# Selective scan of a hybrid layer: building the scan's input from a doubled product, its first column written by ScalarE

## The reference

```python
xz = x @ in_proj_w
xb, zb = jnp.split(xz, 2, axis=-1)
xb = silu(causal_conv4(xb) + conv_b);  zb = silu(zb)
x_dbl = xb @ x_proj_w                 # 128 columns for dt, 16 for B, 16 for C
dt = softplus(dt @ dt_proj_w + dt_proj_b)
decay = jnp.exp(dt[..., None] * A)    # A is [2048 channels, 16 states]
inp = dt[..., None] * Bm[:, :, None, :] * xb[..., None]
h = decay_t * h + inp_t               # recurrence over the 2048 tokens
y = sum_n h * C;  y = y + xb * D
out = (y * zb) @ out_proj_w
```

## Time and profile before

| | us |
|---|---|
| median of 2 runs (6987.1 and 7003.95) | 6995.53 |
| the profiled execution | 7032.75 |
| its span on the slowest core (core 3) | 7031.2 |
| spans of the 8 cores | 6956.0 to 7031.2 |
| first to last scan instruction (starts) | 355.5 to 4000.3 |

### The profile page before, as it was taken

How to read it: one execution, slowest core, us unless ns; L and a number is a source line. 1 busy time by engine, 2 the same in 40 slices (tenths; PEclk the granted TensorE clock), 3 DMA queues, 4 the chain that set the end, 5 groups by cost and what they waited for, 6 DMA issues and landing times.

```text
span 7031.2 us, 35693 instructions; the slowest of 8 cores (6956.0 to 7031.2 us)
## 1 busy us (share of the span) xinstructions
PE 2641.7 (38%) x9120; PEld 949.0 (13%) x9120; DVE 3363.1 (48%) x3380; ACT 1385.9 (20%) x2282; POOL 391.0 (6%) x204
## 2 busy tenths in 40 slices
PE   2322214222114222132111200497833434337978
PEld 1100001000001000010000000143311111113433
DVE  0366673566773666745777540101155565652111
ACT  0122221222221222212222202212110101001120
POOL 1000000000000000000000011000002222120000
PEclk8655556655557555565555555698966666668987
DMA  6400004100002000011000169531400000002313
GB/s 106 73 10 9 2 0 68 36 9 8 0 0 60 23 12 2 0 39 33 0 0 0 24 103 118 85 77 41 91 0 0 0 0 0 0 0 33 75 44 100
DMA packets 691337, 226.18 MB, mean 32 GB/s; under 512 B 680122, under 2 KB 680253, under 8 KB 687552
## 3 DMA queue, kind: packets, MB, share of 16 engines
q1 hardware_dynamic: 555552, 168.14, 10.4%
q0 software_dynamic: 135584, 55.76, 7.1%
HBM read 241.73 MB, written 37.88 MB: 40 GB/s over the span
## 4 chain that ended last, share of the span: by engine, by line
DVE 37%; PE 26%; ACT 14%; DMA 10%; issue 6%; DVEq 4%; POOL 1%; ACTq 1%; SPq 0%; POOLq 0%; PEldq 0%
DVE AR L723 17%; ACT AR L695 10%; PE ps L955 7%; PE ps L925 6%; DVE AR L709 5%; DVE AR L1091 4%; PE ps L470 3%; DVEq L58 3%; DVE AR L1127 3%; PE ps L1154 2%; DVE AR L511 2%; PE ps L308 2%; PE ps L1058 2%; DMA AR<-w 1%; POOL AR L1140 1%
## 5 line engine op out<-in xcount | busy, mean ns | idle before, releaser
L747 PE MATMUL ps<-AR 128*128 128x512 bf16 x1024 | 518.2, 608 | 2459.3 <-DVE AR L739 2459.3
L723 DVE TENSOR_TENSOR_SCAN AR<-AR 128x1024 bf16<-128x1024 f32 x512 | 1173.5, 2292 | 40.0 <-issue 3.1
L695 ACT ACTIVATE AR<-AR 128x511 f32<-128x511 f32 x1024 | 674.1, 705 | 1.6 <-issue 1.1
L709 DVE TENSOR_TENSOR AR<-AR 128x1024 bf16<-128x1024 bf16 x512 | 354.5, 692 | 527.3 <-ACT AR L695 519.4
L925 PE MATMUL ps<-AR 128*128 128x512 bf16 x2048 | 474.7, 395 | 119.7 <-DVE AR L343 111.7
L732 ACT ACTIVATE AR<-AR 128x2 f32<-128x2 bf16 x512 | 104.6, 204 | 1962.4 <-DVEq L63 1962.4
L955 PE MATMUL ps<-AR 128*128 128x512 bf16 x2048 | 471.9, 396 | 14.8 <-DMA AR<-w2s 14.8
L962 DVE TENSOR_SCALAR AR<-ps,AR 128x1024 f32<-128x1024 f32 x32 | 43.0, 1344 | 896.8 <-PE ps L955 896.8
L747 PEld LDWEIGHTS ps<-AR 128*128 128x128 bf16 x1024 | 69.7, 104 | 2897.2 <-issue 2897.2
L1154 PE MATMUL ps<-AR 128*128 128x512 bf16 x512 | 220.5, 586 | 636.4 <-POOL AR L1140 609.6
L739 DVE TENSOR_TENSOR AR<-AR 128x1024 bf16<-128x1024 bf16 x512 | 354.4, 692 | 125.9 <-issue 125.9
(11 more groups left out here) (92 smaller groups left out, 2212.8 us busy)
## 6 DMA issues: line engine op xcount, KB each, us to landing
AR<-w1s SPq DMA_DIRECT2D x128, 256.0 KB, 3.0
AR<-w2s SPq DMA_DIRECT2D x32, 1024.0 KB, 6.6
AR<-ip_bf SPq DMA_DIRECT2D x96, 256.0 KB, 2.9
AR<-bc_hbm SPq DMA_DIRECT2D x4, 4096.0 KB, 14.2
AR<-op_bf SPq DMA_DIRECT2D x24, 512.0 KB, 4.7
X<-x_fm SPq DMA_DIRECT2D x1, 8192.0 KB, 28.6
AR<-in_proj_w POOLq DMA_DIRECT2D x32, 256.0 KB, 5.1
ip_bf<-AR SPq DMA_DIRECT2D x32, 256.0 KB, 3.0
```

Source lines behind the costliest of these rows:

```text
L695: nbase=nbase: e.activation(out=dec_all[gb][:, n, 1:TQ], in_=dt[b][:, 1:TQ], func=AF.Exp, scale=av[:, dd, nbase + n:nbase + n + 1]),
L709: e.tensor_tensor(out=inp_all[0], in0=v[b].unsqueeze(1) .broadcast_to([128, G, TQ]), in1=bbc[:, nbase:nbase + G, :], op=ALU.mult))
L723: e.tensor_tensor_scan(out=h_all[hb].rearrange("p a b -> p (a b)"), data0=dec_all[gb].rearrange("p a b -> p (a b)"), data1=inp_all[0].rear ...
L747: e.matmul(self.bank(b, TQ), self.ident[:], hc_all[hb][:, n, :], start=(ng == 0 and n == 0), stop=(ng == NG - 1 and n == G - 1)),
```

## The change

- `v` becomes `vdup`, [128, 2, 512] in bf16: L664 writes its first half, a drain and a copy (VectorE) write the second. `inp` gets two buffers, used in turn by the parity of the group.
- In the prologue VectorE now waits for `bc_done` ahead of L664. Behind L677 come two more operations of 16 elements, each with drains: `B[0] * v[0]` and its sum with `seedv`. So `seedv` now holds the whole of column 0 for all 16 states.
- In a group the multiplication covers columns 1 to 511 of both states only, with `vdup` and B both plain rows of 511 at an offset of one element. It no longer waits for the decays nor for the carry. The addition of 2 elements and its drain are gone. ScalarE, behind its two Exp, copies two elements of `seedv` into column 0 of `inp`, and the scan waits for that copy alone (`col0_done`), which stands behind the Exp in ScalarE's queue.
- `yv` becomes bf16, so L761 has bf16 operands only.

```diff
-        yv = [self.view(o_yv + i * TQ * 4, F32, [128, TQ]) for i in (0, 1)]
+        yv = [self.view(o_yv + i * TQ * 2, BF16, [128, TQ]) for i in (0, 1)]
...
+                r.wait("ve", "d_spb", bc_done)
                 r.op("ve", lambda e, dd=dd, b=b: e.tensor_tensor(
-                    out=v[b], in0=dt[b], in1=xbs[:, dd, :], op=ALU.mult))
+                    out=vdup[b][:, 0, :], in0=dt[b], in1=xbs[:, dd, :],
+                    op=ALU.mult))
+                r.drain("ve")
+                r.op("ve", lambda e, b=b: e.tensor_copy(
+                    out=vdup[b][:, 1, :], in_=vdup[b][:, 0, :]))
...
-                sv_[b] = r.op("ve", lambda e, dd=dd, b=b: e.tensor_tensor(
+                r.op("ve", lambda e, dd=dd, b=b: e.tensor_tensor(
                     out=seedv[b], in0=dec0s[b],
-                    in1=self.carry[:, dd * 16:dd * 16 + 16], op=ALU.mult),
+                    in1=self.carry[:, dd * 16:dd * 16 + 16], op=ALU.mult))
+                r.drain("ve")
+                r.op("ve", lambda e, b=b: e.tensor_tensor(
+                    out=dec0s[b], in0=bbc[:, 0:16, 0],
+                    in1=vdup[b][:, 0, 0:1].broadcast_to([128, 16]),
+                    op=ALU.mult))
+                r.drain("ve")
+                sv_[b] = r.op("ve", lambda e, b=b: e.tensor_tensor(
+                    out=seedv[b], in0=seedv[b], in1=dec0s[b], op=ALU.add),
                               inc="c_ve")["c_ve"]
+                r.drain("ve")
...
-                    dec_done[key] = ca["c_act"]
-                    r.wait("ve", "c_act", dec_done[key])
+                    r.wait("act", "c_ve", sv_[b])
+                    ca = r.op("act", lambda e, b=b, ib=ib, nbase=nbase:
+                              e.activation(
+                                  out=inp_all[ib][:, :, 0],
+                                  in_=seedv[b][:, nbase:nbase + G],
+                                  func=AF.Copy), inc="c_act")
+                    col0_done = ca["c_act"]
+                    dec_done[key] = col0_done
                     r.wait("ve", "d_spb", bc_done)
-                    if dd + ng > 0:
-                        sem, val = hc_done.get(keyp2, ("c_ve", 0))
-                        r.wait("ve", sem, val)
-                        r.wait("ve", "c_act", carry_done.get(keyp2, 0))
-                    r.op("ve", lambda e, b=b, nbase=nbase:
+                    r.op("ve", lambda e, b=b, ib=ib, nbase=nbase:
                          e.tensor_tensor(
-                             out=inp_all[0],
-                             in0=v[b].unsqueeze(1)
-                             .broadcast_to([128, G, TQ]),
-                             in1=bbc[:, nbase:nbase + G, :],
+                             out=inp_all[ib][:, :, 1:],
+                             in0=vdup[b][:, :, 1:],
+                             in1=bbc[:, nbase:nbase + G, 1:],
                              op=ALU.mult))
                     r.drain("ve")
-                    r.op("ve", lambda e, b=b, nbase=nbase:
-                         e.tensor_tensor(
-                             out=inp_all[0][:, :, 0],
-                             in0=inp_all[0][:, :, 0],
-                             in1=seedv[b][:, nbase:nbase + G], op=ALU.add))
-                    r.drain("ve")
+                    r.wait("ve", "c_act", col0_done)
                     r.op("ve", lambda e, gb=gb, hb=hb, ib=ib:
                          e.tensor_tensor_scan(
```

More of the change, by code:

```diff
@@ L362, in _mamba @@
         o_dt = alloc(2 * TQ * 4)
-        o_v = alloc(2 * TQ * 2)
+        o_vdup = alloc(2 * 2 * TQ * 2)
         o_dec = alloc(2 * 2 * TQ * 4)
-        o_inp = alloc(2 * TQ * 2)
+        o_inp = alloc(2 * 2 * TQ * 2)
         o_h = alloc(2 * 2 * TQ * 2)
@@ L389, in _mamba @@
         dt = [self.view(o_dt + i * TQ * 4, F32, [128, TQ]) for i in (0, 1)]
-        v = [self.view(o_v + i * TQ * 2, BF16, [128, TQ]) for i in (0, 1)]
+        vdup = [self.view(o_vdup + i * 2 * TQ * 2, BF16, [128, 2, TQ])
+                for i in (0, 1)]
         dec_all = [self.view(o_dec + (i % 2) * 2 * TQ * 4, F32, [128, 2, TQ])
                    for i in range(3)]
-        inp_all = [self.view(o_inp, BF16, [128, 2, TQ]) for i in range(3)]
+        inp_all = [self.view(o_inp + i * 2 * TQ * 2, BF16, [128, 2, TQ])
+                   for i in (0, 1)]
         h_all = [self.view(o_h + i * 2 * TQ * 2, BF16, [128, 2, TQ])
@@ L686, in groups @@
                     hb = ng % 2
+                    ib = ng % 2
                     key = (dd, ng)
@@ L693, in groups @@
                     for n in range(G):
[L694 to L700, removed]
@@ L701, in groups @@
-                    dec_done[key] = ca["c_act"]
-                    r.wait("ve", "c_act", dec_done[key])
-                    r.wait("ve", "d_spb", bc_done)
-                    if dd + ng > 0:
-                        sem, val = hc_done.get(keyp2, ("c_ve", 0))
-                        r.wait("ve", sem, val)
-                        r.wait("ve", "c_act", carry_done.get(keyp2, 0))
-                    r.op("ve", lambda e, b=b, nbase=nbase:
+                        r.op("act", lambda e, dd=dd, b=b, gb=gb, n=n,
+                             nbase=nbase: e.activation(
+                                 out=dec_all[gb][:, n, 1:TQ],
+                                 in_=dt[b][:, 1:TQ], func=AF.Exp,
+                                 scale=av[:, dd, nbase + n:nbase + n + 1]))
@@ L714, in groups @@
                              op=ALU.mult))
                     r.drain("ve")
-                    r.op("ve", lambda e, b=b, nbase=nbase:
-                         e.tensor_tensor(
-                             out=inp_all[0][:, :, 0],
-                             in0=inp_all[0][:, :, 0],
-                             in1=seedv[b][:, nbase:nbase + G], op=ALU.add))
-                    r.drain("ve")
-                    r.op("ve", lambda e, gb=gb, hb=hb:
+                    r.wait("ve", "c_act", col0_done)
@@ L723, in groups @@
+                    r.op("ve", lambda e, gb=gb, hb=hb, ib=ib:
                          e.tensor_tensor_scan(
@@ L725, in groups @@
                              data0=dec_all[gb].rearrange("p a b -> p (a b)"),
-                             data1=inp_all[0].rearrange("p a b -> p (a b)"),
+                             data1=inp_all[ib].rearrange("p a b -> p (a b)"),
                              initial=0.0, op0=ALU.mult, op1=ALU.add))
```

## The result

The changed kernel takes 6538.65 us (median of 11 runs, 6525.16 to 6603.42) against 6997.08 us before (10 runs, 6983.12 to 7049.35). The ratio is 0.9339, with a 95% interval of 0.931 to 0.9369: 458 us less by the medians. Its profiled execution took 6518.9 us.

A forecast was written before the change was run, and what follows sets the result against it. A dependency bounds the kernel: VectorE's multiplication waits for ScalarE's decays. 484 inside blocks + 19 between blocks - 45 at quarter starts = 458 us less, giving 6538 us; range 6485 to 6680, eight in ten.

The forecast's parts named there:

- Inside a block: Gap between two scans of a block: 2.91 us falls to 1.83, gaining 1.08 us 448 times, 484 us.
- ScalarE's leg: From a scan's end through carry copy, two Exp and column copy to the next scan: 1.81 us.
- VectorE's leg: From a scan's end through `hc`, the multiplication, drain and waits to the next scan: 1.83 us.
- the multiplication follows after 0.07 for its satisfied wait: On VectorE behind `hc` inside a block: an already satisfied wait costs 0.07 us before the multiplication starts.
- The multiplication's rate: The multiplication over two rows of 511 at an odd offset takes 0.69 us, as L709 did.
- the first rival: Multiplication at one element per cycle because rows start 2 bytes off: 1.23 us, 184 us less, 6812; chance 0.12.
- the third: Rival: the multiplication becomes a slow one, 1.72 us for 1022 elements, 66 us more, 7061; chance 0.03.
- The second rival: Longer handover from Exp through column copy to scan: ScalarE's leg 2.11 us, 332 us less, 6664; chance 0.08.
- From block to block: From L664 to the scan at 60 block changes: 3.62 us falls to 3.30, gaining 19 us.
- Everything up to L664 is as before: At a block change, the stretch ahead of the first product L664 keeps its length, waiting for L658.
- yv in bf16: The gate multiplication L761 may get shorter but gains nothing, since idle time before L664 takes it.
- Start of a quarter: L664 of block 0 now waits for the B and C DMA: 40 us lost in three quarters, 5 in the fourth.

The follow-up runs named there:

- e1: Kernel before, with only the multiplication moved ahead of the wait for the decays; the two-element addition stays on VectorE: 6534.67 us, ratio 0.9333.
- e9: Changed kernel plus seven unused TensorE matmuls behind the seventh group of each of 24 blocks followed by input projections: 6481.16 us, ratio 0.9219.
- e4: Changed kernel with yv in float32 again: 6553.71 us, ratio 0.9328.
- e3: Changed kernel with the wait for B and C moved from a block's first product to behind the layernorm: 6510.15 us, ratio 0.9293.
- e10: Kernel before reordered: decays and multiplication made a group ahead, prologue and projections spread over groups, no doubling copy; second run: 5986.61 us, ratio 0.8563.

## Why the prediction was right

- **The bound.** Right: the wait of the multiplication for the decays. e1 moves that wait alone, without the two for the groups before it, and has the whole gain.
- **Inside a block.** Right in mechanism, 21 us short in size. ScalarE's leg was forecast at 1.81 and is 1.81 (1610.23, the end of one scan, to 1612.03 or 1612.04, the start of the next). VectorE's leg was forecast at 1.83 and is 1.68: the step that failed is "the multiplication follows after 0.07 for its satisfied wait". It starts 0.08 us before `h * C` ends, wait or no wait (1611.08 against 1610.47 + 0.69). So ScalarE decides alone, as the 0.27 us of idle time ahead of the scan says. The sum was also short because the one group of the earlier trace rows, 5.20 us, stands 0.04 us below the mean of before, 5.24, in which 38 distances are some 0.3 us longer.
- **The multiplication's rate.** Forecast 0.69, measured 0.686, so the first rival fell, and the third, which needed 1.59 or more, with it. Of the two pages of the Trainium skill that were weighed, the trace agrees with the Vector Engine (DVE) Microarchitecture Reference, section 5.1 Performance modes: a start 2 bytes off a 4-byte boundary and rows of 511 cost nothing (686 ns for 1022 elements). It does not bear out the 4-byte alignment that the Trainium skill, VectorE: DVE Perf Modes, section "Mode 2×_1P — pack two bf16 into one 32-bit read", asks for.
- **The handover on ScalarE.** The second rival fell: the column copy starts 0.10 us before the Exp ends (1611.74 against 1611.84), and the scan follows its end by 0.11.
- **From block to block.** Wrong in size: 19 us forecast for the 60 seams, 5 measured. Four of the 60 hold no prologue, which the count missed; they gained 0.45 us each. In the other 56, from the first product on, 0.39 us was gained where 0.32 was forecast (the copy took 0.29, not 0.35). The step that failed is "Everything up to L664 is as before". It was the same work, but at 24 seams TensorE did it at a clock that rose later, 0.7 us each; in the others the added wait took 0.07. e9, in which the clock had risen ahead of the projections or rose within 1.1 us of their start, shows that it decides the length of these seams.
- **yv in bf16.** Right for the 56 seams with a prologue: L772 fell to 0.426 us and the path took nothing of it, as e4 shows. In the last seam of each quarter it did, 1.1 us in all.
- **Start of a quarter.** Right: 45 us forecast, 42 measured, and e3 brings 36 back.
- **The sum.** 458 us forecast, 467.5 in the stage, 458 by the medians. That the time, 6538.65 us, came out within 1 us of the 6538 forecast is luck: +21 inside the blocks, -14 at the seams and +3 at the quarters' starts leave 10 us, and the scatter of the runs, which is wider, took these. The terms of the forecast's own range add up to 6480 to 6613 rather than 6485 to 6610, which changes nothing.

## What to carry to other kernels

Look at what stands behind a wait in an engine's queue and ask of each instruction whether it needs that wait: one multiplication moved ahead of it was worth all of this change, and the new buffers, the doubled product and the copy on the second engine added little or cost time. A wait put ahead of work that doesn't need it costs the other way round, 10 to 15 us at the start of three quarters here. And a seam whose work is unchanged can still grow, when TensorE's clock rises later in it.

## What the hardware showed that was not expected

- The granted clock at a seam depends on what TensorE did just ahead of it: the same 16 matmuls took 4.80 us before, 5.92 in the changed kernel, and 3.62 with seven more matmuls ahead of them. Useless matmuls made the kernel faster: ratio 0.9219 (0.9178 to 0.926) against 0.9339 (0.931 to 0.9369).
- A wait that is already satisfied costs VectorE no time that the trace shows between two of its operations; the next starts 0.08 us before the last one's end, as L666 does behind L664 with no wait between them.
- Stages with identical code differ by up to 100 us between executions (2980 to 3085 us behind the last scan), with matmuls of 381 to 411 ns on the mean (L1006 in e10, L951 in e1). An effect under 1% in one stage is better read from that stage than from the whole time.
